# An order table for layer 2 and trace-true durations for the planner

## What is computed

```python
xn = _layernorm(x, axis=-1)
x = x + _L0_attn_ref(xn, ...) + _L0_ffn_ref(xn, ...)
xn = _layernorm(x, axis=-1)
x = x + _L1_attn_ref(xn, ...) + _L1_ffn_ref(xn, ...)
return x

# layer 1 attention: a gated linear recurrence (RWKV-6)
S = jnp.exp(w_t)[..., None] * S + kv
# layer 1 feed-forward: 8 heads a token, 16 experts, top 2, exact gelu
hmid = jax.nn.gelu(jnp.einsum('td,edi->tei', t, W1) + b1, approximate=False)
# layer 2 attention: 16 heads of 8, one shared key and value head, causal
att = jnp.einsum('bthd,bsd->bhts', q, k) * scale
att = jax.nn.softmax(jnp.where(causal[None, None], att, -jnp.inf), axis=-1)
# layer 2 feed-forward: 8 SwiGLU experts, top 2, run in two loops over z
z = z + mixed.reshape(B, S, D)
```

## Time and profile before

| | us |
|---|---|
| median of 3 runs | 1351.98 (1349.23 to 1352.38) |
| span of the profiled execution | 1317.6 |
| median less span | 34.4 |
| layer 1, from 40 to the barrier | about 507.5 |
| layer 2, from the barrier at 547.5 | 770.1 |
| PE busy, DVE, ACT, POOL (share of span) | 92%, 80%, 68%, 37% |
| PE busy in layer 2 | 723.19 |

### The profile page before, as it was taken

The page is one execution under the profiler, slowest core; times in us unless marked ns, Lnnn a source line. Parts: engine busy times, 40 slices in busy tenths (PEclk is TensorE's granted clock), DMA queues, the critical chain, the costliest instruction groups (busy, mean ns, idle before and its releaser), DMA issues. The chain is left out here.

```text
span 1317.6 us, 28397 instructions
## 1 busy us (share of the span) xinstructions
PE 1206.5 (92%) x11172; PEld 593.3 (45%) x11172; DVE 1050.7 (80%) x1954; ACT 891.2 (68%) x1246; POOL 482.3 (37%) x446
## 2 busy tenths in 40 slices
PE   6888998899988989798899999999899999999988
PEld 3333332333433323365555555555456544555434
DVE  4589789869898779769977799778787798787863
ACT  3668997898877888643266676666666666666666
POOL 3542554345514872320155511555025550000170
PEclk8889998999999999989999999999999999999999
DMA  6333322233332343248364544556335453233020
GB/s 224 116 117 125 106 94 101 92 109 101 100 103 94 111 132 106 93 118 233 106 183 136 174 122 117 151 139 157 87 101 160 133 142 89 72 82 105 19 64 28
DMA packets 129876, 152.88 MB, mean 116 GB/s; under 512 B 16048, under 2 KB 90800, under 8 KB 129616
## 3 DMA queue, kind: packets, MB, share of 16 engines
q1 hardware_dynamic: 111104, 127.50, 32.9%
q0 software_dynamic: 8192, 16.79, 4.3%
q10 hardware_dynamic: 10448, 6.77, 1.7%
HBM read 109.20 MB, written 41.81 MB: 115 GB/s over the span
## 5 line engine op out<-in xcount | busy, mean ns | idle before, releaser
L2887 ACT ACTIVATE ax_prob<-second_pair 128x1024 f32<-128x1024 f32 (+1 forms) x320 | 292.9, 939 | 146.4 <-PE second_pair L2840 94.4
L528 ACT ACTIVATE m_act_h<-first_pair,const 128x1024 f32<-128x1024 f32 x256 | 270.1, 1114 | 57.7 <-PE first_pair L482 44.1
L2764 DVE TENSOR_REDUCE am_top<-second_pair 128x2 f32<-128x1024 f32 (+1 forms) x192 | 222.9, 1175 | 38.6 <-PE second_pair L2718 25.5
L3019 POOL DMA_INDIRECT slot_tokens<-xn,mr_slots x128 | 124.0, 969 | 273.7 <-PE second_bank L1877 86.2
L3049 POOL DMA_INDIRECT m_back<-slot_results,mr_slots x128 | 122.2, 955 | 243.2 <-PE second_pair L2718 167.7
L482 PE MATMUL first_pair<-m_terms,w1s 96*128 96x512 bf16 x512 | 145.9, 391 | 19.6 <-ACT m_act_h L528 19.4
L2826 PE MATMUL ax_sums<-ax_prob,al_vs 128*32 128x512 f32 (+3 forms) x1536 | 161.2, 500 | 1.8 <-ACT ax_prob L2887 1.6
L494 PE MATMUL first_pair<-m_act_h,const 128*32 128x512 f32 x1024 | 130.4, 610 | 7.0 <-DVE m_prod L543 4.9
L582 POOL TENSOR_TENSOR m_both<-m_prod,m_both 128x512 f32<-128x512 f32 x64 | 86.7, 1371 | 123.8 <-DVE m_both L543 123.8
L2863 PE MATMUL second_pair<-al_qs,al_ks 51*128 51x512 bf16 (+3 forms) x768 | 115.9, 329 | 12.8 <-DVE am_top L2764 4.3
L2718 PE MATMUL second_pair<-al_ks,al_qs 48*128 48x512 bf16 (+3 forms) x768 | 116.2, 327 | 7.6 <-DVE am_top L2764 3.7
(11 more groups left out here) (396 smaller groups left out, 2515.1 us busy)
## 6 DMA issues: line engine op xcount, KB each, us to landing
m_wt<-in_experts SPq DMA_DIRECT2D x96, 384.0 KB
m_share<-shares SPq DMA_DIRECT2D x128, 256.0 KB
m_rows<-slot_tokens SPq DMA_DIRECT2D x60, 128.0 KB
slot_results<-m_y SPq DMA_DIRECT2D x60, 128.0 KB
stack<-mp_part SPq DMA_DIRECT2D x48, 128.0 KB
m_terms<-stack SPq DMA_DIRECT2D x64, 96.0 KB, 3.7
qstack<-ap_qpart SPq DMA_DIRECT2D x48, 128.0 KB
al_qs<-qstack SPq DMA_DIRECT2D x32, 192.0 KB, 3.9
```

What stands on the lines that cost most here:

```text
L528: A.activation(self.act_h[:, slot, :, :], banks.bank("up", n, ep)[:, :, :], ACT.Gelu, bias=self.w("b1", 4 * half + ep, 4 * half + ep + 1)) ...
L2764: V.tensor_reduce(into[:, 2 * a:2 * a + 2, at], tile[:, :, 0:n], AX, ALU.max, negate=True).then_inc(*banks.empties("max", i, m))
L2887: A.activation(dst, src, ACT.Exp, scale=SCALE).then_inc(*banks.empties("sum", i, u))
L3019: G.indirect_dma_start(self.tokens[g], bass.IndirectOffsetOnAxis(ap=self.route.slots[g][second][:, i:i + 1], axis=0), self.entry.zn(GC * g ...
```

## The change

`Plan.run` takes an optional table that spells, for each engine, from which stream the next step comes (one letter a step). With a table the wishes and the patience no longer decide anything; the forward play only gives start times and banks. Layer 2 gets such a table (1595 steps on PE, 772 on DVE, 735 on ACT, 229 on POOL, 353 on SP), layer 1 does not. Besides, about forty planned durations are set to other values, in both layers. Two planned needs are added in layer 2; they add no wait to the program.

```diff
-    def run(self):
-
+    def run(self, orders=None):
+
+        spelled = collections.defaultdict(list)
+        for engine, stream in self.streams:
+            spelled[engine].append((engine, stream))
+        turns = {engine: [spelled[engine][NAMES.index(name)] for name in order] for engine, order in (orders or {}).items()}
+        taken = collections.Counter()
...
             for (engine, stream), n in heads.items():
+                if orders and turns[engine][taken[engine]] != (engine, stream):
+                    continue
...
-            engine = min(best, key=lambda e: min(best[e])[0])
+            engine = min(sorted(best, key=ENGINES.index), key=lambda e: min(best[e])[-1] if orders else min(best[e])[0])
+            taken[engine] += 1
...
+FIRST_ORDERS = None
+SECOND_ORDERS = {
+    "PE":
+        "babkalkcllmlcdmmfkmnfkoloeelnlnlmdnmbkmnlmbonlkomnmnoclocknllmldmfendkmnmenlggnlnmggmfkggkllgllnngmmmmkmggnngnggllgmgngggoggmgkkllngnllhmmmkn"
...
-    return p.run(), p
+    return p.run(FIRST_ORDERS), p
...
-        dve("low", ("mixed", it, s), at, 1.24, ("delta", it, s), *([("low", it, 0, 1)] if s else ago("state", NC)), port=True)
+        dve("low", ("mixed", it, s), at, 0.68, ("delta", it, s), *([("low", it, 0, 1)] if s else ago("state", NC)), port=True)
...
-    pe("levels", ("lev", it, 0), at, 2.2, ("self", it, NH - 1), *ago("fill_a"), lag=0.3, fills=1, uses=[("lev", it, 0, s) for s in range(2)])
+    pe("levels", ("lev", it, 0), at, 1.12, ("self", it, NH - 1), *ago("fill_a"), lag=0.3, fills=1, uses=[("lev", it, 0, s) for s in range(2)])
...
-    return p.run(), p
+    return p.run(SECOND_ORDERS), p
...
-        dve("turn", ("parts", i), end, 1.6, ("rows", i), *([("sent", i - 2)] if i > 1 else []))
+        dve("turn", ("parts", i), end, 1.05, ("rows", i), *([("sent", i - 2)] if i > 1 else []))
```

More of the change, by code:

```diff
@@ L1 @@
+import collections
 import functools
@@ L2065 @@
 TILE_SWITCH, TABLE_SWITCH = 0.1, 1.3
+ENGINES = ["PE", "ACT", "DVE", "POOL", "SP"]
+NAMES = "abcdefghijklmnopqrstuvwxyzABCDEFGHIJKLMNOPQRSTUVWXYZ"
 class Plan:
@@ L2256, in plan_units @@
             if half:
-                pool("pair", ("pair", pair, j), at + DOWN_AFTER, 1.3, ("product", n, j))
+                pool("pair", ("pair", pair, j), at + DOWN_AFTER, 1.26, ("product", n, j))
         if n % 4 == 3:
@@ L2296, in plan_mixtures @@
         free += [("elog", c) for c in WINDOW if WINDOW[c] < it]
-        pe("hidden", ("hid", it, s), at, 0.93, ("mix", it, 1, s), *free, lag=0.25, fills=1)
+        pe("hidden", ("hid", it, s), at, 0.88, ("mix", it, 1, s), *free, lag=0.25, fills=1)
         act("hidden", ("hidc", it, s), at, 0.5, ("hid", it, s), *free, lag=0.2, frees=("hid", it, s), table="ge")
@@ L2342, in plan_levels @@
     for half in range(2):
-        pe("levels", ("lev64", it, half), at, 1.25, ("scale", it, 64, 2), lag=0.3, fills=1, uses=[("lev64", it, half, s) for s in range(2)])
+        pe("levels", ("lev64", it, half), at, 0.97, ("scale", it, 64, 2), lag=0.3, fills=1, uses=[("lev64", it, half, s) for s in range(2)])
         for s in range(2):
@@ L2478, in plan_attention @@
         free += [("weigh", NG * (b - 1) - 1, steps - 1)] if g == 0 and b > 1 else []
-        sp("load", ("load", i), slot_at(max(i - 0.8, 0.0)), 1.0 if g else 2.4, *([("send", 2 * b), ("send", 2 * b + 1)] if g == 0 else []), *free, lag=2.8)
+        sp("load", ("load", i), slot_at(max(i - 0.8, 0.0)), 1.0 if g else 2.4, *([("send", 2 * b), ("send", 2 * b + 1)] if g == 0 else []), *([] if i else [("zero",)]), *free, lag=2.8)
         for u, (blk, pairs, seg, n) in enumerate(MAX_USES):
             wish = slot_at(i + MAX_SHIFT + u / len(MAX_USES))
-            pe("max", ("max", i, u), wish, score[n] * len(pairs) + (0.08 * len(pairs) if seg == blk // 4 else 0.0), ("load", i), lag=0.32, fills=2)
+            pe("max", ("max", i, u), wish, score[n] * len(pairs) + (0.08 * len(pairs) if seg == blk // 4 else 0.0), ("load", i), ("cast",), lag=0.32, fills=2)
             dve("top", ("top", i, u), wish, longest[n], ("max", i, u),
@@ L2522, in plan_route @@
             dve("route", ("zn", ph, c), at, 1.1, ("invert", ph))
[L2523 removed]
+        pe("route", ("turned", ph, c), at, 0.5, ("zn", ph, c) if loop else ("scale", GC * g + c), *before, lag=0.25, fills=1)
         act("route", ("turnedc", ph, c), at, 0.48, ("turned", ph, c), *before, frees=("turned", ph, c))
```

79 lines of the change are left out of this document (56 added, 23 removed).

## The result

The kernel after takes 1340.54 us (median of 14 runs, 1336.56 to 1348.31), the kernel before on the same chip 1351.89 (14 runs, 1344.2 to 1360.16). The ratio is 0.9922, 95% interval 0.9899 to 0.9945: 11.4 us less. Forecast were 28 us less, 1324; the range, 1300 to 1345, holds the time.

A forecast was written before the change was run, and what follows sets the result against it. The prediction took layer 2 to be bound by PE, with no engine standing out in layer 1. It summed 12 + 11 + 2 + 3 = 28 us less, from 1352.0 to 1324 us, with a range of 1300 to 1345.

The forecast's parts named there:

- 34 us outside the span: Whole kernel: the median lies 34.4 us above the profiled span, and that part stays untouched by the change.
- Part 1: PE in layer 2: 720 changes of matmul shape become 659, 12 us less busy time.
- Part 2: PE's waits in layer 2: more PE work between filler and waiter, 11 us less, bounds 0 and 20.
- 20 us, if the idle time before `max` and `sum` goes altogether: PE in layer 2: upper bound of the gain from waits, from 20.4 us of idle time there.
- Rival 2: Layer 2: hidden waits from in-order queues go too, 54 us less in all, 1298 us; chance 0.14.
- Part 3: Start of layer 2: weight loads no longer behind two sends on SP, 2 us less.
- Part 4: Layer 1: one table load fewer, a changed tail and more even work, 3 us less, bounds 8 either way.
- a fourth of the 13 us of better evenness is a gain: Middle of layer 1: work spread more evenly between the `up`s, estimated 3 us less.
- The tail: End of layer 1: 3.4 us less behind the last gelu, 4.6 more on ACT ahead, 1.2 us more.
- Rival 3: Layer 1 loses more than layer 2 gains as `up` and `gelu` block each other, 1358 us; chance 0.07.
- Rival 1: Layer 2: only fewer shape changes pay, PE's waits close up elsewhere, 12 us less, 1340; chance 0.20.
- Rival 4: Layer 2: fixed order is brittle, varying DMA landings stop PE more often, 1347 to 1356 us; chance 0.07.

The follow-up runs named there:

- e9: Kernel after with layer 1's order as before (the program of e3), on a slower chip: 1316.14 us, ratio 0.9704 of the kernel before.
- e6: Kernel before with only PE's order in layer 2 changed at 43 places, 655 shape changes in place of 720: 1353.54 us, ratio 1.0000.
- e10: e9 with PE's layer 2 order changed at 32 places, 607 shape changes in place of 659: 1319.90 us, ratio 0.9733 of the kernel before.
- e11: e9 with PE's layer 2 order changed at 31 places, 711 shape changes in place of 659: 1321.73 us, ratio 0.9752 of the kernel before.
- e1: Kernel before, unchanged, run again for a second trace on a fast chip: 1322.69 us, ratio 1.0001.
- e2: Kernel after, unchanged, on the same fast chip as e1: 1293.32 us, ratio 0.9791 of the kernel before.
- e4: Kernel before with layer 1's new durations and order, layer 2 as before, on a fast chip: 1337.63 us, ratio 1.0113.
- e3: Kernel after with layer 1's order as before, layer 2's table and durations kept, on a fast chip: 1280.32 us, ratio 0.9679 of the kernel before.
- e7: Kernel before with only the planner's rule for ties between engines changed in layer 1, old durations, on a slower chip: ratio 1.0238.

## Why the prediction was wrong, point by point

- **The base.** The sum was made on a trace of a fast chip and set against a median from a slower one, with a reason (34 us outside the span) that no row showed. On fast chips the change gives -28.4 and -24.9 us, on the chip of the result -11.4. There the forecast's 25 us of gain in layer 2 met some 40 (39.7 in e9), and its 3 us of gain in layer 1 met a loss of some 28, by subtraction.
- **Part 1, PE's own work, -12: mechanism right, size wrong.** 61 changes fewer at the measured 0.096 are 5.9 us of busy time, half of the 12. The prices were read at single spots of the timeline. Of these 5.9 us an unknown part reaches the end: 0 in e6, 0.058 of 0.096 in layer 2 of e10 and e11, and less in their medians. The sign named for it, PE busy at 710 to 712, nearly came true (712.4), but for another reason, below.
- **Part 2, waits, -11: far too small.** On one chip, idle time in layer 2 fell by 23.3 us (46.3 to 23.0). PE's busy time fell by 17.4, of which shapes explain about 6, and the granted clock some 2 (0.993 in place of 0.989, at 6 us for 0.01). The other 9 are likely short waits under the tail of a matmul: a matmul of 0.38 us is followed after 0.22, so up to 0.16 us of waiting still counts as busy. That is argued, not shown. If it is so, some 32 us of waits went in all. What failed here is the bound "20 us, if the idle time before `max` and `sum` goes altogether": it left out the idle time of the other groups and what hides in the busy time. The same part had counted 82 us lost to waits, of which distance forces 25. Rival 2 took half of the other 57 as well, 12 + 11 + 28 = 51 for layer 2; the truth, 41, lies between it and the forecast of 25.
- **Part 3, the start, -2: right.** In the first 52.5 us of layer 2 PE idles for 8.1 us in e1 and 5.4 in e2, in the first 100 us for 14.6 and 11.4. There is no `m_wt` wait of 1.6 us any more, and the first `top` comes 49.3 us into layer 2 in place of 55.6.
- **Part 4, layer 1, -3: wrong in sign, and the step that failed.** It came out at +13 to +16 on fast chips, some +28 on the slower one. The bounds were 8 us either way, "a seventh of ACT's idle" time; that idle time grew by 20 us (57.2 to 77.4). The step "a fourth of the 13 us of better evenness is a gain" judged an order by a sum over neighbouring `up`s, and no number read from a plan (its end, the DVE work beside POOL work) ranked the orders here. The tail went half as thought: from the 225th gelu to the last it takes 52.6 us in e4 in place of 48.0 in e1, the +4.6 forecast for the group norm ahead of the gelus. From the last gelu's start to layer 2 it takes 13.6 us in e4 in place of 15.2 in e1, and 14.9 in e2 in place of 16.6 in e3, so 1.6 or 1.7 less where 3.4 were expected. That makes 3 us of loss in the tail. The other 12 of e4's 15.3 lie before it, where `up` and gelu wait for each other; why this order makes them wait more stays open, see the rule for ties above.
- **Rivals.** Rival 3 named the right place and mechanism, `up` and gelu blocking each other, with ACT's idle time as its measure. It had a chance of 0.07 only because it was priced as an alternative to the gain of layer 2 and not as a term beside it. Rival 1 (1340, 12 us less) gives the measured time by luck, and not its reason: it has waits of PE that stay and a layer 1 that costs nothing. Rival 4 did not show: PE waits for DMAs for 1.0 us in layer 2 of e2, 0.9 in e3, and 6.2 in e1.

The best version is neither kernel: e3, the table of layer 2 with layer 1 left alone, 0.9679 of before on a fast chip and 0.9704 on a slower one.

## What to carry to other kernels

An edit that feeds better numbers to a scheduler also gives a new order, which may cost more than the numbers bring: run a control whose edit carries no information, here a rule for ties, before a gain or loss is put down to the numbers. One such control is not enough, and it should not stand in all the other runs as well, or it can't be told from them. Take a change apart by stages and keep the parts that pay, and once a stage has an order that measures well, write it down as a table where a planner's edit can't reach it. And look whether the profile's own time agrees with the median beside it before a sum is made on it.

## What the runs showed of the hardware

Chips differ by 2.3 to 2.7% for the same program (1321 to 1352 or 1356 us for the kernel before). The durations of single ACT and DVE instructions agree to a few ns (e3 and e9). Two differences show. The mean granted clock over all runs of the kernel before is 0.974 on both fast chips (17 and 13 runs) and 0.966 and 0.967 on two slower ones (28 and 11 runs); in single traces the two kinds overlap. And on the slower chips all engines stand still at once for a while. Timeline of e9, all engines:

```profile
1293.47 0.95 POOL L3101 DMA_INDIRECT m_back<-slot_results,mr_slots  x1 [0.31 <-issue]
...
1293.56 0.39 PE L2915 MATMUL second_pair<-al_qs,al_ks 51*128 51x512 bf16 x2
1295.53 1.02 ACT L2939 ACTIVATE ax_prob<-second_pair 128x1024 f32<-128x1024 f32 x1 [2.69 <-remote]
1295.66 0.69 DVE L3017 TENSOR_TENSOR x<-second_bank,x 128x512 f32<-128x512 f32 x1 [19.17 <-remote]
1295.90 0.95 POOL L3101 DMA_INDIRECT m_back<-slot_results,mr_slots  x1 [1.48 <-remote]
...
1296.61 0.39 PE L2915 MATMUL second_pair<-al_qs,al_ks 51*128 51x512 bf16 x2 [2.66 <-ACT ax_prob L2939]
```

PE ends the scores at 1293.95, and ACT starts to read them at 1295.53; POOL, which has nothing to do with them and issues every 1.25 us elsewhere, pauses too. In e9 six such pauses of PE, ACT and DVE together, 4.3 us in all, lie in layer 2 after its first 600 us. Every one of the nine traces from slower chips has two to six there, none of the nine from fast chips has one (e1 has one of 1.2 us earlier). They stand in layer 1 too: four in e9 between 468 and 482 us of the span, 2.9 us in all, and one of 4.6 us in e7. They are only a part of the loss: between 437 and 452 us of layer 1, e9 falls 8.5 us behind e3, which runs the same program, and between 650 and 706 us of layer 2 another 15.5 us. What causes them stays open.
